# Cross-attention and expert feed-forward: the product with v in float32 on four 32-column strips, with a separate order of steps for each engine

## The chip, the core and the metric

The kernel runs on one core of a Trainium2 chip. The metric is the device time of one execution in microseconds (us). Engines are named as the profile names them: PE is TensorE (PEld its weight loads), DVE VectorE, ACT ScalarE, POOL GpSimd, SP SyncE, which here only issues DMAs (SPq). SBUF is the on-chip memory that all engines read, PSUM the banks that PE writes its results into.

## What is computed

There are 16 batches of 128 tokens of width 256, 2048 tokens in all. The reference, cut to what matters:

```python
# attention: 16 heads of width 16; one k and one v (each 128 x 16 per batch) shared by all heads
qh = (norm(x) @ w_q) ...;  k, v = split(ctx @ w_kv)
attn_prob = softmax(einsum('bhid,bjd->bhij', qh, k) / sqrt(16))
out = einsum('bhij,bjd->bhid', attn_prob, v);  x1 = x + out @ w_concat
# feed-forward on the normed x1: top-1 of 8 experts (256 -> 1024 -> 256), capacity 256 tokens,
# beside a residual MLP (256 -> 1024 -> 256) for every token, mixed by a softmax of two coefficients
out = res_mlp(a) * coef[:, :1] + moe(a) * coef[:, 1:] + residual
```

## The kernel before, in words

The tokens are worked in 8 units of 256 (two batches, t = 0 and 1), then the 8 experts follow. For every unit the kernel transposes ctx and the normed x (L586), makes kv and q (L591), splits q and k in three bfloat16 parts, sends them through DRAM to lie stacked (qstack, kstack), and computes the scores twice: A (L644, heads on the free axis, for the row maximum, which DVE reduces at L957) and B (L666, keys on the partitions, with the maximum subtracted by two added rows of the stack).

B comes in 8 groups per unit (g = 0 to 7; four heads and one batch each, one PSUM bank of 128 x 512). ACT takes the exponential of each group twice: in float16 into `p_hi` (L824) and in float32 into `p32` (L825; the profile calls it p). DVE subtracts the two into a float16 `p_lo` (L949, `low_part`). PE then multiplies p with v in `weigh` (L680 and L681): for each of the four heads of a group, `p_hi` and then `p_lo` is the stationary operand (128 x 128) and `vparts` the moving one, 49 columns wide (three bfloat16 parts of v and a column of ones, which gives the softmax's sum). Two groups fill one bank `pbank`; DVE takes the reciprocal of the ones' column (L973), sums the three parts (L974) and scales into `o_rows` (L977, function `o`). When the unit's four such pieces are done, PE transposes `o_rows` (oT, L586), ACT copies it, PE multiplies with w_concat (proj, L591 with wc), and DVE adds to x (L984), so that layer norm, gate and the residual MLP can follow.

The residual MLP of a unit (`up`, L591 with w1r, with the gelu on ACT at L860; `down`, L751 with w2r) runs one unit behind, between the attention steps of the next unit. A unit with such MLP work beside it is called loaded below (units 2 to 7 have nearly all of it). The experts have the same two products with w1e and w2e. Float32 products appear in the profile as two PE records for each 128 x 128 by 128 x 256 product, so that "x8" is four products.

All engines take their steps from one list, `plan`: each step has a time made of its unit's start (`OWN`, 32 apart from unit 3) and a phase from the tables `AT0`, `AT1` and `AT`, and the list sorted by time is the program order of each engine. The times are only for sorting. What really holds a step back are semaphores: `weigh` waits for `p_lo`; ACT's exponentials of group k wait for `p_lo` of group k-2 (L824, two buffers of `p32`); a PSUM bank is claimed again only when its last user has been read (`FREED`), and A and B share the two banks `sbank`.

Of the kernel before, what the change touches and what calls it, by code (L numbers as in the profile page):

```python
# [5 lines left out]
def xattn_moe_ffn_kernel(nc, x, ctx, w_q, w_kv, w_c, nw, nb, wg, inter_w, inter_b, output_w, output_b,  # L6
# [10 lines left out]
    P = 128  # L17
# [7 lines left out]
    T = 2  # L25
# [12 lines left out]
    NPS = 6  # L38
    VW = 3 * DH + 1
# [18 lines left out]
    OWN = [0.0, 14.83, 38.9, 67.3]  # L58
    while len(OWN) < U + 3:
# [3 lines left out]
        "load": [-77.76], "ln1": [-59.31], "xn": [-52.55], "ctxT": [-55.73], "xT": [-42.22], "kv": [-39.7],  # L63
        "q": [-39.27], "qrest": [-41.07], "qmid": [-34.81], "qlast": [-36.41], "vt": [-38.49],
        "A": [-16.51, -16.37, -14.32, -14.04, -12.48, -10.82, -10.55, -9.8], "M": [-12.87, -8.44],
        "B": [-1.47, -0.38, 0.52, 3.42, 7.22, 7.91, 10.76, 12.78],
        "low": [-0.31, 1.72, 3.41, 7.68, 9.19, 10.26, 11.63, 13.03],
        "PV": [4.6, 6.47, 8.23, 10.22, 11.82, 14.03, 15.29, 17.85], "o": [6.72, 9.53, 12.45, 15.99], "oT": [18.92],
        "proj": [20.34], "ln2": [22.4], "core": [23.87], "gate": [29.59], "loc": [37.82], "gw": [2.43],
        "bias": [12.71], "up": [18.3, 19.06, 22.25, 25.8],  # L70
        "down": [-1.64, -0.04, 0.29, 3.05, 5.91, 6.8, 10.19, 12.71], "kspill": [-35.6],
        "qspill": [-43.69, -43.49, -43.39], "gather": [-35.16, -34.04],
    }
    AT1 = {
        "load": [-99.55], "ln1": [-62.15], "xn": [-50.95], "ctxT": [-42.13], "xT": [-37.91], "kv": [-40.31],
        "q": [-34.66], "qrest": [-40.27], "qmid": [-28.41], "qlast": [-34.73], "vt": [-30.21],
        "A": [-19.69, -17.73, -15.68, -14.01, -13.84, -12.18, -11.91, -11.52], "M": [-10.41, -9.7],
        "B": [-0.63, 1.24, 4.13, 4.57, 7.09, 8.2, 10.89, 12.79],
        "low": [0.72, 2.0, 3.73, 7.82, 9.64, 10.74, 12.14, 13.85],
        "PV": [3.94, 5.82, 7.6, 9.61, 12.75, 13.45, 14.73, 17.31], "o": [6.44, 9.98, 13.29, 17.32], "oT": [18.38],  # L80
        "proj": [19.72], "ln2": [21.77], "core": [23.95], "gate": [26.61], "loc": [39.06], "gw": [14.41],
        "bias": [19.65], "up": [15.33, 16.98, 19.62, 23.21],
        "down": [-0.9, 1.35, 1.75, 5.08, 8.54, 10.31, 13.7, 20.67], "kspill": [-40.35],
        "qspill": [-42.52, -35.18, -34.88], "gather": [-34.05, -33.21],
# [13 lines left out]
    EARLY = 0.01  # L98
    LOADS = {
        "late": [-70.79], "vec": [-39.4], "zero": [-46.04, -45.13, -6.03, -0.66],  # L100
        "weights": [0.5, 14.17, 14.73, 27.03, 27.11],
    }

    HALVES = [T] + [1] * (U - 1)
# [1008 lines left out]
```

## Time and profile before

| | us |
|---|---|
| median of 3 runs (lowest, highest) | 441.46 (439.79, 446.71) |
| the profiled execution | 442.74 |
| its span, first to last instruction | 440.1 |
| PE busy (matmul records) | 372.5 |
| DVE busy | 202.7 |
| ACT busy | 190.1 |
| POOL busy | 158.2 |
| mean granted TensorE clock, share of full speed | 0.92 |

Busy time of PE counts a matmul until its last result has landed, which overlaps the next one. For what a matmul costs the queue, the distance between two starts is read, not the duration.

### The profile page before, as it was taken

To read this page: it belongs to the slowest core of one execution; us is meant where nothing else is said; L and a number is where in the kernel's file an instruction comes from. 1 tells how busy PE (TensorE), PEld (TensorE's weight loads), DVE (VectorE), ACT (ScalarE), POOL (GpSimd) and SP (SyncE) were. 2 spreads that over 40 slices of the span, in tenths; PEclk is the share of its full clock that TensorE was granted. 3 is DMA by queue.
4 is the path that set the end of the run, shared out by engine and by line. 5 is a ranking of instruction groups with operands and counts; after the bars stand their busy time and mean duration, and the time that the engine had idled before them with its cause. 6 is when DMAs were issued, how large, how long until landed. Compare 5 with 4: busy or idle time off the path is not lost. (4 is left out here: it accounts for less than half of the span.)

```text
span 440.1 us, 6595 instructions
## 1 busy us (share of the span) xinstructions
PE 372.5 (85%) x2298; PEld 298.4 (68%) x2298; DVE 202.7 (46%) x612; ACT 190.1 (43%) x373; POOL 158.2 (36%) x219
## 2 busy tenths in 40 slices
PE   4758676867998799899899879879999999999992
PEld 2435444655776677677677767768888888888881
DVE  3255778838545965965955957521001110101110
ACT  3213474557246646546546628443143322332210
POOL 4322134238174068168168061265002121212122
PEclk9865658989699999899899999989999999999997
DMA  6567670231023362472402400193213586571212
GB/s 200 182 181 218 216 184 18 74 82 38 15 72 116 98 227 74 113 255 75 106 24 73 108 26 15 42 370 92 56 41 96 167 246 189 136 220 13 24 18 30
DMA packets 51336, 49.84 MB, mean 113 GB/s; under 512 B 4764, under 2 KB 48488, under 8 KB 51304
## 3 DMA queue, kind: packets, MB, share of 16 engines
q1 hardware_dynamic: 48232, 45.21, 33.7%
q0 software_dynamic: 3072, 4.21, 5.2%
q8 instruction: 18, 0.29, 0.3%
q14 instruction: 14, 0.11, 0.1%
HBM read 33.65 MB, written 15.63 MB: 112 GB/s over the span
## 5 line engine op out<-in xcount | busy, mean ns | idle before, releaser
L860 ACT ACTIVATE h<-ubank,vecT 128x256 f32<-128x256 f32 x128 | 53.7, 471 | 129.3 <-PE ubank L591 129.1
L751 PE MATMUL mbank<-w2r,h 128*128 128x256 f32 x256 | 66.1, 399 | 0.5 <-ACT h L860 0.5
L591 PE MATMUL ubank<-ao,w1r 128*128 128x256 f32 x256 | 63.8, 396 | 0.0
L559 POOL DMA_INDIRECT out_rows<-yrow,rowid x16 | 24.8, 1550 | 103.3 <-DVE yrow L1078 73.2
L751 PE MATMUL mbank<-w2e,h 128*128 128x256 f32 x256 | 60.8, 379 | 0.0
L591 PE MATMUL ubank<-ao,w1e 128*128 128x256 f32 x256 | 60.0, 379 | 0.0
L751 PEld LDWEIGHTS mbank<-w2r,h 128*128 128x128 f32 x256 | 49.4, 198 | 7.6 <-issue 0.6
L591 PEld LDWEIGHTS ubank<-ao,w1r 128*128 128x128 f32 x256 | 49.5, 200 | 6.6
L591 PEld LDWEIGHTS ubank<-ao,w1e 128*128 128x128 f32 x256 | 48.5, 190 | 6.6
L751 PEld LDWEIGHTS mbank<-w2e,h 128*128 128x128 f32 x256 | 48.2, 190 | 6.3
L949 DVE TENSOR_TENSOR p_lo<-p,p_hi 128x512 f16<-128x512 f32 x64 | 46.4, 738 | 11.9 <-ACT p L825 11.7
L824 ACT ACTIVATE p_hi<-sbank 128x512 f16<-128x512 f32 x64 | 38.4, 600 | 30.1 <-PE sbank L666 17.5
L1074 DVE TENSOR_TENSOR ytmp<-mbank,outb 128x256 f32<-128x256 f32 x16 | 6.8, 425 | 90.9 <-PE mbank L751 90.9
L957 DVE TENSOR_REDUCE smax<-sbank 128x4 f32<-128x512 f32 x64 | 41.5, 682 | 11.6 <-PE sbank L644 9.8
L825 ACT ACTIVATE p<-sbank 128x512 f32<-128x512 f32 x64 | 38.4, 601 | 0.0
L680 PE MATMUL pbank<-vparts,p_hi 128*128 128x49 bf16 x256 | 24.0, 194 | 13.1 <-DVE p_lo L949 12.7
L644 PE MATMUL sbank<-kstack,qstack 96*128 96x128 bf16 x256 | 26.0, 244 | 10.7 <-ACT p L825 4.4
L680 PEld LDWEIGHTS pbank<-vparts,p_hi 128*128 128x128 f16 x256 | 19.1, 102 | 23.4 <-DVE p_lo L949 13.9
L644 PEld LDWEIGHTS sbank<-kstack,qstack 96*128 96x128 bf16 x256 | 19.0, 109 | 18.6 <-DVE smax L957 7.1
L666 PE MATMUL sbank<-qstack,kstack 98*128 98x512 bf16 x64 | 27.0, 431 | 4.0 <-DVE smax L957 2.6
L591 PE MATMUL mbank<-xT,wq 128*128 128x256 f32 x64 | 20.5, 476 | 4.0 <-ACT ao L841 3.0
L527 POOL TENSOR_TENSOR coef<-ge,grec 128x2 f32<-128x2 f32 x8 | 1.6, 202 | 61.6 <-DVE grec L1053 61.6
(127 smaller groups left out, 517.4 us busy)
## 6 DMA issues: line engine op xcount, KB each, us to landing
w1e<-in_L_ffn_inter_w SPq DMA_DIRECT2D x8, 1024.0 KB, 5.8
w2e<-in_L_ffn_output_w SPq DMA_DIRECT2D x8, 1024.0 KB, 8.8
qstack<-dram_q SPq DMA_DIRECT2D x16, 384.0 KB, 4.5
dram_q<-qpart SPq DMA_DIRECT2D x8, 384.0 KB, 2.6
dispatched<-zrow SPq DMA_DIRECT2D x4, 516.0 KB, 5.2
drow<-dispatched SPq DMA_DIRECT2D x8, 258.0 KB, 3.6
xs<-in_x SPq DMA_DIRECT2D x8, 256.0 KB, 3.4
ctxs<-in_ctx SPq DMA_DIRECT2D x8, 256.0 KB, 3.6
```

The costliest lines, as they stand in the source:

```text
L559: pool.indirect_dma_start(out=out[:, :], in_=yrow[:, e % 2, t, :], in_offset=None, compute_op=ALU.add, out_offset=bass.IndirectOffsetOnAxi ...
L591: last = nc.tensor.matmul(dst, w[kc], v[kc], start=(kc == 0), stop=(kc == len(w) - 1))
L644: last = nc.tensor.matmul(b[:, i * P:(i + 1) * P], qstack[0:KS, r, t, 4 * (g % HG) + i, :], kstack[0:KS, r, bs], start=True, stop=True)
L666: nc.tensor.matmul(b[:, :], kstack[:, r, bs], qstack[:, r, t, hs:hs + 4, :], start=True, stop=True)\
L680: nc.tensor.matmul(dst, p_hi[:, k % NPS, i, :], v, start=True, stop=False)
L751: last = nc.tensor.matmul(b[:, 0:D], h[:, n % 2, f, t * P:(t + 1) * P], w2[:, f, :], start=(f == 0), stop=(f == FC - 1))
L824: nc.scalar.activation(p_hi[:, k % NPS, :, :], scores, ACT.Exp, scale=SCALE).then_inc(sem("p_hi"), 1)
L825: nc.scalar.activation(p32[:, k % 2, :, :], scores, ACT.Exp, scale=SCALE).then_inc(sem("b_exp"), 1)
L860: nc.scalar.activation(h[:, n % 2, f, :], place["up", n, c][:, j, :], ACT.Gelu_apprx_tanh, bias=vecT[:, col:col + 1]).then_inc(sem("gelu_d ...
L949: V.tensor_tensor(p_lo[:, k % NPS, :, :], p32[:, k % 2, :, :], p_hi[:, k % NPS, :, :], ALU.subtract)\
L957: V.reduce_max(smax[:, g // HG, hs:hs + 4], place["A", u, g][:, :].rearrange("p (h t) -> p h t", h=4), AX)\
L1074: V.tensor_tensor(ytmp[:, t, :], b, outb[:, e, :], ALU.add).then_inc(sem("down_read"), 1)
```

## The change

The product with v no longer uses parts. ACT takes one exponential per group, in float32; `low_part` and its DVE subtraction are gone, as are the bfloat16 parts of v: `vone` holds v in float32, 32 columns wide (16 of v, one of ones, 15 of zeros). `weigh` is now called once per batch t, when its four groups of p are there: four float32 products, with `vone` (128 x 32) stationary and one group of p (128 x 512) moving, each at its own 32-column strip of the array (`tile_position=(0, 32 * g)`), so that group g's result lies in partitions 32g to 32g+31 of one bank. The result has head and token on the free axis. ACT copies it to `o_raw` (new step on ACT), and PE turns it back with four float32 transposes of 128 x 128 (new step `part`). DVE takes one reciprocal per batch and one multiplication straight from PSUM into `o_rows`. POOL's `bias` has one wait more, on a semaphore that POOL itself raises earlier in its order.

Besides, every engine sorts the list for itself: `order(lag)` adds to each kind of step a small number of that engine (`LAG_PE`, `LAG_ACT`, ...). A few phases in the tables are also changed; of the tables the diff below shows two lines.

```diff
-        "low": [-0.08, 0.18, 3.63, 7.8, 9.64, 10.74, 12.14, 13.57],
-        "PV": [4.11, 5.98, 7.74, 9.73, 12.42, 13.54, 14.8, 17.36], "o": [4.91, 9.92, 13.48, 16.76], "oT": [18.72],
+        "PV": [5.63, 14.29], "part": [7.43, 16.09], "o": [7.83, 16.49], "oT": [17.79],
...
-    plan = [step for _, _, step in sorted(steps)]
+    def order(lag):
+        return [step for _, _, step in sorted((place + lag.get(step[0], [0.0])[0], n, step) for place, n, step in steps)]
...
-                pe.wait_ge(sem("p_lo"), k + 1)
-                v = vparts[:, u % 3, g // HG, :]
-                for i in range(4):
-                    dst = b[:, 4 * (g % 2) + i, 0:VW]
-                    nc.tensor.matmul(dst, p_hi[:, k % NPS, i, :], v, start=True, stop=False)
-                    last = nc.tensor.matmul(dst, p_lo[:, k % NPS, i, :], v, start=False, stop=True)
+            def weigh(u, t):
+                n = T * u + t
+                pe.wait_ge(sem("b_exp"), HB * (n + 1))
+                if t == 0:
                     pe.wait_ge(sem("v_ready"), u + 1)
+                b = claim("PV", u, t)
+                for g in range(HB):
+                    last = nc.tensor.matmul(b[32 * g:32 * g + 32, :, :], vone[:, u % 3, t, :], p32[:, n % 2, g, :, :],
+                                            start=True, stop=True, tile_position=(0, 32 * g))
                 last.then_inc(sem("pv_done"), 1)
+
+            def o_part(u, t):
+                n = T * u + t
+                b = claim("part", u, t)
+                pe.wait_ge(sem("o_copied"), n + 1)
+                for i in range(HB):
+                    last = nc.tensor.transpose(b[:, i, :], o_raw[:, n % 2, i, :], ident[:, :])
+                last.then_inc(sem("o_turned"), 1)
...
-                if k >= 2:
-                    act.wait_ge(sem("p_lo"), k - 1)
-                if k >= NPS:
-                    act.wait_ge(sem("pv_done"), k - NPS + 1)
-                scores = place["B", u, g][:, :].rearrange("p (h t) -> p h t", h=4)
-                nc.scalar.activation(p_hi[:, k % NPS, :, :], scores, ACT.Exp, scale=SCALE).then_inc(sem("p_hi"), 1)
-                nc.scalar.activation(p32[:, k % 2, :, :], scores, ACT.Exp, scale=SCALE).then_inc(sem("b_exp"), 1)
+                if k >= 2 * HB and g % HB == 0:
+                    act.wait_ge(sem("pv_done"), k // HB - 1)
+                scores = place["B", u, g][:, :].rearrange("p (h t) -> p h t", h=HB)
+                nc.scalar.activation(p32[:, (k // HB) % 2, g % HB, :, :], scores, ACT.Exp, scale=SCALE)\
+                    .then_inc(sem("b_exp"), 1)
+
+            def o_copy(u, t):
+                n = T * u + t
+                act.wait_ge(sem("pv_done"), n + 1)
+                if n >= 2:
+                    act.wait_ge(sem("o_turned"), n - 1)
+                copy(o_raw[:, n % 2, :, :], place["PV", u, t][:, :, :]).then_inc(sem("o_copied"), 1)
...
-            def low_part(u, g):
-                k = G * u + g
-                dve.wait_ge(sem("b_exp"), k + 1)
-                dve.wait_ge(sem("p_hi"), k + 1)
-                V.tensor_tensor(p_lo[:, k % NPS, :, :], p32[:, k % 2, :, :], p_hi[:, k % NPS, :, :], ALU.subtract)\
-                    .then_inc(sem("p_lo"), 1)
...
-                own(V.reciprocal(o_rec[:, r, :], bank[:, :, VW - 1]))
-                V.tensor_reduce(o_sum[:, r, :, :], bank[:, :, 0:3 * DH].rearrange("p h (a d) -> p h d a", a=3), AX,
-                                ALU.add).then_inc(sem("o_summed"), 1)
-                dve.wait_ge(sem("o_summed"), G // 2 * u + b + 1)
-                V.tensor_tensor(o_rows[:, t, r * P:(r + 1) * P].rearrange("p (h d) -> p h d", d=DH),
-                                o_sum[:, r, :, :], o_rec[:, r, :].unsqueeze(2).broadcast_to([P, NH // 2, DH]), ALU.mult)\
+                b = place["part", u, t][:, :, :].rearrange("p i (j x) -> p j i x", j=HB)
+                V.reciprocal(o_rec[:, :, :], b[:, :, :, DH]).then_inc(sem("o_root"), 1)
+                dve.wait_ge(sem("o_root"), n + 1)
+                V.tensor_tensor(o_rows[:, t, :].rearrange("p (j i d) -> p j i d", j=HB, i=HB), b[:, :, :, 0:DH],
+                                o_rec[:, :, :].unsqueeze(3).broadcast_to([P, HB, HB, DH]), ALU.mult)\
                     .then_inc(sem("o_ready"), 1)
```

The first place is PE in a steady unit, where the scores B (`sbank<-qstack,kstack`) alternate with the MLP's second product (`mbank<-w2r,h`). Before, with only the first pair of the product with v of a group of four pairs:

```order
L666 MATMUL sbank<-qstack,kstack 128x512
L680 MATMUL pbank<-vparts,p_hi 128x49
L681 MATMUL pbank<-vparts,p_lo 128x49
...
L666 MATMUL sbank<-qstack,kstack 128x512
L751 MATMUL mbank<-w2r,h 128x256 x2
L680 MATMUL pbank<-vparts,p_hi 128x49
L681 MATMUL pbank<-vparts,p_lo 128x49
```

and now, from the last two scores of the first batch to those of the second:

```order
L687 MATMUL sbank<-qstack,kstack 128x512 x2
L776 MATMUL mbank<-w2r,h 128x256 x2
L697 MATMUL pbank<-p,vone 32x512 x4
L687 MATMUL sbank<-qstack,kstack 128x512
L776 MATMUL mbank<-w2r,h 128x256 x2
L706 MATMUL pbank<-ident,o_raw 128x128 x4
...
L687 MATMUL sbank<-qstack,kstack 128x512
L697 MATMUL pbank<-p,vone 32x512 x4
L776 MATMUL mbank<-w2r,h 128x256 x2
L665 MATMUL sbank<-kstack,qstack 128x128 x8
```

Eight small pieces of the product with v, one after each group, have become two large ones, each behind the last group of its batch, and each followed by a set of transposes after one or two other steps.

The second place is ACT in the same unit: before (four of the eight pairs),

```order
L824 ACT_TABLE_LOAD
L824 ACTIVATE p_hi<-sbank 128x512
L825 ACTIVATE p<-sbank 128x512
...
L850 ACTIVATE ge<-gd 128x20
L860 ACT_TABLE_LOAD
```

and now:

```order
L847 ACT_TABLE_LOAD
L847 ACTIVATE p<-sbank 128x512 x4
L791 ACTIVATE o_raw<-pbank 128x512
L847 ACTIVATE p<-sbank 128x512 x4
L791 ACTIVATE o_raw<-pbank 128x512
L880 ACTIVATE ge<-gd 128x20
L890 ACT_TABLE_LOAD
```

Sixteen exponentials have become eight, and two copies have come in between; the copy of the first batch stands in front of the exponentials of the second, and the copy of the second in front of the gelu of the MLP.

## Rows read from the trace of the kernel before

**Rows 1.** Busy time by stretch: engine busy (instructions), PEclk, DMA share, GB/s.
```profile
core 0: us, PE busy (x) PEld busy (x) DVE busy (x) ACT busy (x) POOL busy (x), PEclk, DMA share, GB/s
...
40.00:67.00 27.00, 20.11 (x142) 12.71 (x141) 17.66 (x41) 14.77 (x29) 7.26 (x8) 0.58 0.74 219
...
91.00:131.00 40.00, 32.11 (x220) 25.29 (x219) 23.35 (x74) 21.21 (x39) 22.39 (x33) 0.87 0.20 55
...
163.00:195.00 32.00, 28.78 (x214) 22.60 (x212) 22.20 (x69) 17.90 (x35) 16.93 (x24) 0.95 0.49 152
195.00:227.00 32.00, 28.86 (x216) 22.91 (x215) 21.97 (x67) 18.65 (x36) 16.59 (x24) 0.95 0.25 71
...
308.00:440.00 132.00, 121.77 (x576) 105.81 (x574) 14.41 (x41) 35.06 (x81) 24.80 (x16) 0.98 0.40 103
```

**Rows 2.** PE's timeline, projection of units 3, 4 and 6: start us, us.
```profile
157.16 1.95 PE L591 MATMUL mbank<-wc,oT 128*128 128x256 f32 x8
...
190.20 1.95 PE L591 MATMUL mbank<-wc,oT 128*128 128x256 f32 x8
...
254.45 1.95 PE L591 MATMUL mbank<-wc,oT 128*128 128x256 f32 x8
```

**Rows 3.** PE's timeline in unit 5: start us, us, records, [idle before <-releaser].
```profile
202.41 1.06 PE L591 MATMUL mbank<-wg_raw,ao 128*128 128x10 f32 x8
203.33 1.11 PE L751 MATMUL mbank<-w2r,h 128*128 128x256 f32 x4
...
211.07 0.19 PE L680 MATMUL pbank<-vparts,p_hi 128*128 128x49 bf16 x1
...
211.27 0.38 PE L666 MATMUL sbank<-qstack,kstack 98*128 98x512 bf16 x1
211.49 1.03 PE L751 MATMUL mbank<-w2r,h 128*128 128x256 f32 x4
213.64 0.18 PE L680 MATMUL pbank<-vparts,p_hi 128*128 128x49 bf16 x1 [1.13 <-DVE p_lo L949]
...
215.02 0.20 PE L680 MATMUL pbank<-vparts,p_hi 128*128 128x49 bf16 x1 [0.80 <-DVE p_lo L949]
...
220.44 0.61 PE L644 MATMUL sbank<-kstack,qstack 96*128 96x128 bf16 x8
220.89 0.61 PE L586 MATMUL mbank<-ident,o_rows 128*128 128x128 f32 x4
221.34 1.89 PE L591 MATMUL ubank<-ao,w1r 128*128 128x256 f32 x8
223.07 0.39 PE L644 MATMUL sbank<-kstack,qstack 96*128 96x128 bf16 x4
```

**Rows 4.** PE's groups: busy us, mean ns | idle before, us, by releaser.
```profile
L644 PE MATMUL sbank<-kstack,qstack 96*128 96x128 bf16 x256 | 26.0, 244 | 10.7 <-ACT p L825 4.4 <-DVE smax L957 3.6 <-DMA qstack<-dram_q 2.1
L680 PE MATMUL pbank<-vparts,p_hi 128*128 128x49 bf16 x256 | 24.0, 194 | 13.1 <-DVE p_lo L949 12.7
...
L591 PE MATMUL mbank<-xT,wq 128*128 128x256 f32 x64 | 20.5, 476 | 4.0 <-ACT ao L841 3.0 <-ACT xT L766 0.8 <-issue 0.2
...
L591 PE MATMUL mbank<-ctxT,wkv 128*64 128x256 f32 x32 | 10.9, 475 | 1.4 <-ACT ctxT L766 1.4
```

**Rows 5.** DVE's groups, the same columns.
```profile
L949 DVE TENSOR_TENSOR p_lo<-p,p_hi 128x512 f16<-128x512 f32 x64 | 46.4, 738 | 11.9 <-ACT p L825 11.7
...
L974 DVE TENSOR_REDUCE o_sum<-pbank 128x128 f32<-128x384 f32 x32 | 16.1, 503 | 0.0
...
L977 DVE TENSOR_TENSOR o_rows<-o_sum,o_rec 128x128 f32<-128x128 f32 x32 | 9.6, 301 | 1.1
```

**Rows 6.** ACT's groups, the same columns.
```profile
L825 ACT ACTIVATE p<-sbank 128x512 f32<-128x512 f32 x64 | 38.4, 601 | 0.0
L824 ACT ACTIVATE p_hi<-sbank 128x512 f16<-128x512 f32 x64 | 38.4, 600 | 30.1 <-PE sbank L666 17.5 <-issue 11.9 <-DVE p_lo L949 0.4
...
L766 ACT ACTIVATE oT<-mbank 128x512 f32<-128x512 f32 x8 | 4.8, 597 | 3.0 <-PE mbank L586 2.8
```

More of the change, by code:

```diff
@@ L106, in xattn_moe_ffn_kernel @@
         "period": 17.22, "up": [-2.35, 2.53, 4.67, 9.02],
-        "down": [17.14, 18.77, 20.43, 21.32, 23.56, 25.83, 26.3, 28.47], "ein": [9.47], "first": [-3.51],
+        "down": [17.16, 18.79, 20.45, 21.34, 23.58, 25.85, 26.32, 28.49], "ein": [9.47], "first": [-3.51],
     }
@@ L130, in xattn_moe_ffn_kernel @@
             add(OWN[u] + at["M"][i], "M", u, i + HALVES[u] - T)
-        for kind in ("A", "B", "low", "PV", "o"):
+        for kind in ("A", "B", "PV", "part", "o"):
             for i, phase in enumerate(at[kind]):
@@ L264, in xattn_moe_ffn_kernel @@
         ubank = [ex.enter_context(nc.psum_tensor(f"ubank{i}", [P, 2, UT], f32)) for i in range(2)]
-        pbank = [ex.enter_context(nc.psum_tensor(f"pbank{i}", [P, NH // 2, 64], f32)) for i in range(2)]
+        pbank = [ex.enter_context(nc.psum_tensor(f"pbank{i}", [P, HB, P], f32)) for i in range(2)]
         sems = {}
@@ L306, in uses @@
             if kind == "PV":
-                return [("p", "PV", k[0], k[1] // 2)] if k[1] % 2 == 0 else []
+                return [("p", "PV") + k]
+            if kind == "part":
+                return [("p", "part") + k]
             return []
         place, before_it, held = {}, {}, {ring: [] for ring in RING}
-        for step in plan:
+        for step in order(LAG_PE):
             for ring, *key in uses(*step):
@@ L438, in _ @@
                      "down": down, "end": end}
-            for step in plan:
+            for step in order(LAG_SP):
                 if step[0] in calls:
@@ L568, in _ @@
                      "gw": scatter, "bias": bias, "down": down, "end": end}
-            for step in plan:
+            for step in order(LAG_POOL):
                 if step[0] in calls:
@@ L756, in _ @@
             calls = {"vec": vectors, "ctxT": tr_ctx, "xT": tr_x, "kv": kv, "q": q, "vt": vt, "A": score_max,
-                     "M": max_rows, "B": scores_T, "PV": weigh, "oT": oT, "proj": proj, "core": cT, "gate": lg,
+                     "M": max_rows, "B": scores_T, "PV": weigh, "part": o_part, "oT": oT, "proj": proj, "core": cT, "gate": lg,
                      "loc": loc, "ein": ein, "up": up, "down": down}
-            for step in plan:
+            for step in order(LAG_PE):
                 if step[0] in calls:
```

120 lines of the change are left out of this document (61 added, 59 removed), and 6 rows, old and new, of tables (AT, AT0, AT1).

## The prediction

> **What bounds the kernel now.** I read the busy time by stretch first [rows 1]. In the expert stage (308 to 440) PE is busy 121.77 of 132 us and DVE and ACT are nearly idle; the change touches nothing there, so whatever it is worth arises before 308. In the steady units (163 to 227) PE is busy 28.8 of 32 us, DVE 22, ACT 18. Early on (40 to 67) PE's clock is 0.58 of full, DVE has 17.66 of 27 us and ACT 14.77: there no engine is full, and chains of waits set the pace.
>
> A busy PE is not a full PE, so next I count what a loaded unit takes of PE's queue, from distances between starts [rows 3]. Eight float32 records of 256 columns start over 1.73 us (221.34 to 223.07), 0.216 us each; a unit has 84 of them (32 up, 32 down, 8 q, 8 projection, 4 kv): 18.1 us. Eight groups of B at 0.22 (211.27 to 211.49) are 1.8. Two groups of A take 0.45 (220.44 to 220.89), eight 1.8. A set of four transposes takes 0.45 (220.89 to 221.34), and there are four sets: 1.8. The gate takes 0.9 (202.41 to 203.33), small things some 0.3. The product with v takes 0.20 per group (211.07 to 211.27, eight matmuls), 1.6 per unit. Sum: 26.3 us. The projection of unit 3 starts at 157.16 and that of unit 6 at 254.45 [rows 2], so a unit takes 32.4 us. PE therefore loses 6.1 us per unit in waits and at half clock (the two steady stretches have a mean clock of 0.95; a tenth of the time at half speed costs up to 1.6 us of 32).
>
> Where does it lose them? At the product with v above all: PE waits 13.1 us at L680 over the run, 12.7 of it for `p_lo`, and 4.4 at L644 for ACT's second exponential [rows 4]. In unit 5 two such waits show 1.13 and 0.80 us, and each is really longer by about 0.16, because a matmul's record (0.18) outlasts its place in the queue (0.025) [rows 3]. I put 3.0 us of a unit's 6.1 at these places; about 3.1 lie elsewhere.
>
> **The change part by part.** *Removed.* PE: 64 small matmuls, -1.6 us per unit. ACT: 64 exponentials of 600 ns, -38.4 us over the run [rows 6]. DVE: 64 subtractions, -46.4, and the sums of the parts, -16.1; the scalings go from 32 of 301 ns to 16 larger ones read from PSUM, about even [rows 5]. DVE and ACT aren't full in the steady units, so this counts only through PE's waits: the chain from a group of scores to its product was exponential, exponential, subtraction (0.6 + 0.6 + 0.74) and becomes one exponential.
>
> *Added on ACT.* 16 copies of 128 x 512; the copy of oT, of the same shape, takes 597 ns: 9.6 us over the run [rows 6]. A copy waits for the product with v, and four exponentials (after the first) or the gelus (after the second) are queued behind it. Between product and transposes PE has a group of B and two records' worth of other work or more (0.22 + 0.86 us, from starts 0.22 and 0.216 apart), against 0.16 + 0.60 and two semaphores for the copy: I cost it at nothing. Without this cover it would be about 0.9 us, twice per unit.
>
> *Added on PE: transposes.* Two sets of four at 0.45: +0.9 us per unit [rows 3].
>
> *Added on PE: the strips.* This term decides. A group is one product of 512 columns in float32, two records, each twice as long as one of 256 columns (0.216): 0.43. That the stationary operand is narrow saves nothing by itself: kv's product with 64 columns has a mean of 475 ns, q's with 128 has 476 [rows 4]. So a batch, four strips and eight records, takes 8 x 0.43 = 3.45 us if the strips run one after another. If all four run at once it is 2 x 0.43 = 0.86. No row shows two strips at work together. Between the ends lies a third value. Both records of a product need the same strip, so the second must follow the first; and PE's records start in the order of the program everywhere in the timeline. Then the first record of strip 1 can run beside the second of strip 0, and so on: 5 x 0.43 = 2.15 us per batch. I take this one, 4.3 us per unit, and keep 1.7 and 6.9 as ends.
>
> [...]
>
> *Change of array shape.* Going into and out of the strips may cost PE a pause, four times a unit. The trace has nothing like it; below by 0, above by one matmul's tail, 0.16 each, 0.6 per unit. I take 0.3. [...]
>
> *Waits that remain at the product.* Before each batch's product PE waits for the last exponential: from the start of a group of B, 0.38 until it is done, 0.6 for ACT, 0.1 for semaphores, less what PE does meanwhile (0.22, or 0.22 + 0.86): about 0.9 for the second batch and 0.3 for the first, 1.2 per unit. They replace the 3.0.
>
> *A loaded unit:* -1.6 + 0.9 + 4.3 + 0.3 - 3.0 + 1.2 = +2.1 us. Six of them: +12.6.
>
> *Half clock.* It stands behind PE's waits for `p_lo` in both steady stretches [rows 1]. With fewer waits and more matmul time some of it goes: up to 1.6 us in each of the two, and more in 91 to 131 (mean 0.87). I take -4 (0 to -7).
>
> *Units 0 and 1.* Here DVE and ACT carry the chains. Per unit 8 x 0.74 of DVE and 8 x 0.60 of ACT go, 10.7 us of work, while PE gets its longer product at about half clock, 2 x (4.3 - 0.8) us, in a stretch where it has room. Net per unit -2.5 (between -5 and +3): -5.
>
> *The orders.* DVE loses some 8 us of work per unit, so the maxima and layer norms that PE waits for (3.6 us at L644 alone [rows 4]) come sooner; the new tables shift steps by tenths of a microsecond. No row prices that: nothing at one end, those 3.6 us and as much again at other places at the other. I take -4.
>
> *Sum:* 12.6 - 4 - 5 - 4 = -0.4. Against the profiled execution's 442.74 us, of which 440.1 are span and 2.6 lie around it, this gives 442.3; that run was 1.3 above the median of the runs shown, so 441.0. No change that a measurement would tell: 2% is 8.8 us, about what the measurement of this kernel can tell from none.
>
> **The rivals.** *All strips at once.* A batch takes 0.86 and not 2.15: 2.6 us per unit less, and +2.1 becomes -0.5. Six units: -3; clock -4, early units -6 and orders -4 as above; the sum is -17 and the time 425. As less of PE's work is then there to cover the copy and the chains of layer norm and gate, I give back 3: 428. For it speaks that four strips share no cell of the array and write different partitions; against it, that the second record of a product has to follow its first. No row decides it. [...]
>
> *Strips one after another*, the case in which the change doesn't do what it says. A batch takes 3.45: +1.3 twice, +4.7 per unit, but longer products also cover waits (-0.5): +4.2 x 6 = 25. Early units +2 (their products at half clock are 6.9 us each, and ACT's copy with the exponentials behind it waits for them), clock -2, orders -4: +21, 463. It decides from about 2.7 us per batch on: then PE's added work outweighs all that the waits gave. For it speaks that every product in the trace runs alone.
>
> *ACT's queue turns into the wait.* If the copy comes late, PE stands at the transposes and the exponentials behind it come late too: 0.9 us twice per unit over six units, +11 on my sum: 452. Against it: ACT is busy 18 of 32 us.
>
> **How the numbers follow.** My forecast 0.40, all at once 0.32, one after another 0.18, ACT's queue 0.10. Of the forecast (433 to 450) 0.05 is faster by over 2%, 0.31 within, 0.04 slower. All at once gives 0.28 faster and 0.04 within; one after another 0.17 slower, 0.01 within; ACT's queue 0.06 slower, 0.04 within. Together: faster 0.33, same 0.40, slower 0.27. The forecast's own range is 433 to 450; with the other cases the range is 424 to 463.
>
> **What would show it.** In the profile after: starts of the eight records of a batch's product. Mine: the pairs overlap, some 2.15 us from the first to the next instruction; 0.86 or 3.45 would show a rival. The transposes' wait for ACT's copy should be near nothing; the wait at L680 (13.1) should shrink to some 1.2 us per unit; the projections of units 3 to 6 should lie about 32 us apart; the expert stage should keep its 132 us. The prediction is wrong if a batch's product isn't near 2.15, or if the units shorten though it is.

## The result, and the profile after

The change made no difference of 2%: the kernel after takes 444.89 us (median of 20 runs, 443.27 to 448.85), the kernel before 443.46 (20 runs, 438.38 to 451.54). The ratio is 1.0085, with a 95% interval of 1.0055 to 1.0115, so it is a little slower, and not faster. The ratios here leave out executions more than 1.5% above the fastest of their kernel, seven of the 20 of before and none of after; by the medians of all 20 the kernel after is 0.3% slower. I had forecast 441.0, that is 442.3 for the profiled execution; that one took 447.72, with a span of 446.0. The profiled execution after lies 2.8 us above its own median, the one before 0.7 below, so of the 5.0 us between the two profiled executions only 1.4 are left between the medians. What follows is therefore read from stretches at full clock, not from the spans alone.

The answer to [rows 1] and to the totals:

```profile
core 0: us, PE busy (x) PEld busy (x) DVE busy (x) ACT busy (x) POOL busy (x), PEclk, DMA share, GB/s
40.00:67.00 27.00, 20.50 (x88) 9.53 (x86) 9.21 (x25) 9.50 (x18) 6.91 (x9) 0.68 0.67 198
91.00:131.00 40.00, 33.93 (x185) 25.92 (x184) 15.92 (x58) 17.54 (x31) 18.96 (x29) 0.87 0.20 55
163.00:195.00 32.00, 28.40 (x176) 21.15 (x174) 16.10 (x51) 16.01 (x30) 16.53 (x24) 1.00 0.38 119
195.00:227.00 32.00, 28.40 (x169) 20.76 (x168) 14.85 (x50) 16.01 (x30) 14.63 (x23) 0.95 0.35 103
```
```profile
PE 381.6 (86%) x1978; PEld 292.7 (66%) x1978; DVE 142.2 (32%) x461; ACT 167.6 (38%) x325; POOL 153.2 (34%) x219
```

DVE lost 60 us of work over the run (202.7 to 142.2) and ACT 22 (190.1 to 167.6), as the diff says. In the steady stretches DVE went from 22 to 15 or 16 us of 32. Neither was the bound, and the time did not follow them.

The product with v is what my forecast turned on. PE's timeline in unit 5 of the kernel after (start us, us, records, [idle before <-releaser]), to be laid beside [rows 3]:

```profile
213.67 1.03 PE L776 MATMUL mbank<-w2r,h 128*128 128x256 f32 x4
214.79 1.06 PE L697 MATMUL pbank<-p,vone 128*32 128x512 f32 x8
215.78 0.39 PE L687 MATMUL sbank<-qstack,kstack 98*128 98x512 bf16 x1
216.01 1.03 PE L776 MATMUL mbank<-w2r,h 128*128 128x256 f32 x4
216.88 0.60 PE L706 MATMUL pbank<-ident,o_raw 128*128 128x128 f32 x4
...
219.58 0.38 PE L687 MATMUL sbank<-qstack,kstack 98*128 98x512 bf16 x1
220.65 1.06 PE L697 MATMUL pbank<-p,vone 128*32 128x512 f32 x8 [0.69 <-ACT p L847]
221.64 1.13 PE L776 MATMUL mbank<-w2r,h 128*128 128x256 f32 x4
```

A batch's product, four strips and eight records, takes 0.99 us from its first start to the next instruction (214.79 to 215.78, 220.65 to 221.64; the raw starts give 0.998 and 0.995). It is neither my 2.15 nor the serial 3.45. The raw starts of the eight records in this batch are 214.787, 214.793, 214.800 and 214.807, and then 215.240, 215.247, 215.253 and 215.260: the first records of all four products, 7 ns apart, then the second records of all four. (The records name no strip; that they divide like this is read from the run with one strip below.)

So PE's work per unit grew by only -1.6 + 0.9 + 2 x 0.99 = +1.3 us. Yet a steady unit at full clock became longer. Before, the projections of units 5 and 6 start at 223.29 and 254.45: 31.16 us, a unit without a half-clock stretch. (The 32.4 us of my forecast was a mean over three units, two of which have one.) After, with the places of the waits:

```profile
159.29 1.97 PE L612 MATMUL mbank<-wc,oT 128*128 128x256 f32 x8 [0.62 <-ACT oT L791]
192.25 1.97 PE L612 MATMUL mbank<-wc,oT 128*128 128x256 f32 x8 [0.57 <-ACT oT L791]
226.90 1.97 PE L612 MATMUL mbank<-wc,oT 128*128 128x256 f32 x8 [0.57 <-ACT oT L791]
```

From 226.90 to the next projection at 259.87 it is 32.97 us, 1.8 more than before. (From 159.29 to 259.87 it is 33.5 on the average, where I had expected about 32.) PE's waits by what was waited for (us in total, times, longest) show a new one, for ACT's copy of oT, which had stood nowhere in PE's groups before:

```profile
PE mbank L607 <- DVE core L1021: 10.3, 8, 3.3
PE pbank L697 <- ACT p L847: 7.8, 9, 1.8
PE sbank L665 <- DVE smax L977: 6.7, 9, 2.1
...
PE mbank L612 <- ACT oT L791: 4.2, 6, 1.1
```

Against [rows 4], the product's waits have fallen from 13.1 to about 8 us, but those for the maxima at A have grown from 3.6 to 6.7, and 4.2 us for oT are new. The timeline after shows why. After the last product, PE now runs through this piece of its order:

```profile
225.26 0.63 PE L607 MATMUL mbank<-ident,o_rows 128*128 128x128 f32 x4
225.72 0.61 PE L665 MATMUL sbank<-kstack,qstack 96*128 96x128 bf16 x8
226.90 1.97 PE L612 MATMUL mbank<-wc,oT 128*128 128x256 f32 x8 [0.57 <-ACT oT L791]
228.71 1.89 PE L612 MATMUL ubank<-ao,w1r 128*128 128x256 f32 x8
230.43 0.61 PE L665 MATMUL sbank<-kstack,qstack 96*128 96x128 bf16 x8
231.61 0.40 PE L665 MATMUL sbank<-kstack,qstack 96*128 96x128 bf16 x4 [0.56 <-DVE smax L977]
231.84 0.61 PE L607 MATMUL mbank<-ident,ctxs 128*128 128x128 f32 x4
...
236.54 0.63 PE L607 MATMUL mbank<-ident,core 128*128 128x128 f32 x4 [0.69 <-DVE core L1021]
```

Between the transposes of o_rows and the projection stand only two groups of A (0.45 us), too little to cover ACT's copy of 0.6 us (0.597 in [rows 6]); before, eight records of the up-projection (1.73 us) and one group of A stood there [rows 3]. And with the projection earlier, twelve matmuls of A (three groups, on two banks) follow in a row, so PE waits for a maximum. DVE, whose order is fixed too, adds a delay of its own (same columns; L1003 adds to x, L1021 makes core):

```profile
228.91 0.69 DVE L1003 TENSOR_TENSOR xs<-xs,mbank 128x512 f32<-128x512 f32 x1 [1.47 <-PE mbank L612]
230.86 1.29 DVE L977 TENSOR_REDUCE smax<-sbank 128x4 f32<-128x512 f32 x2 [1.27 <-PE sbank L665]
232.06 0.74 DVE L926 BATCH_NORM_STATS2 stats<-xs 128x6 f32<-128x256 f32 x2
...
234.44 0.69 DVE L977 TENSOR_REDUCE smax<-sbank 128x4 f32<-128x512 f32 x1 [0.49 <-PE sbank L665]
235.05 1.35 DVE L1021 TENSOR_SCALAR core<-xs,mv,yy 128x256 f32<-128x256 f32 x2
```

The layer norm of the new x waits behind maxima whose scores come later: from the addition to x to the second core it takes 6.6 us (228.91 to 235.51; the raw start of the second is 235.51). In the kernel before it took 4.1 (225.27 to 229.33). The two instructions for core also last longer here, 0.54 and 0.88 us against 0.40 and 0.41 before; what that goes with shows further down. So the order of the steps, which I had put down as a gain of 4 us, became the suspect.

### The profile page after: what moved, and what is told of

Its sections match the earlier page's. It is cut to its first block, busy times and chain, and to the rows that moved or that the text cites. A ratio compares the mean times of both kernels' runs of the same rounds, so it can differ in the third digit from the quotient of the medians.

```text
span 446.0 us, 5656 instructions
## 1 busy us (share of the span) xinstructions
PE 381.6 (86%) x1978; PEld 292.7 (66%) x1978; DVE 142.2 (32%) x461; ACT 167.6 (38%) x325; POOL 153.2 (34%) x219
## 4 chain that ended last, share of the span: by engine, by line
PE 65%; DMA 10%; ACT 8%; DVE 7%; issue 5%; POOL 2%; SPq 2%; DVEq 0%; POOLq 0%; ACTq 0%
PE mbank L776 20%; PE ubank L612 18%; PE mbank L612 11%; DMA drow<-dispatched 8%; PE mbank L607 4%; PE pbank L697 4%; ACT p L847 3%; PE sbank L665 3%; PE sbank L687 3%; DVE smax L977 3%; PE pbank L706 2%; DVE core L1021 2%; ACT h L890 1%; DMA wq_raw<-in_L_xattn_w_q 1%; ACT oT L791 1%
## 5 line engine op out<-in xcount | busy, mean ns | idle before, releaser
L776 PE MATMUL mbank<-w2r,h 128*128 128x256 f32 x256 | 64.1, 390 | 0.5 <-ACT h L890 0.5
L612 PE MATMUL ubank<-ao,w1r 128*128 128x256 f32 x256 | 62.7, 393 | 0.0
L776 PEld LDWEIGHTS mbank<-w2r,h 128*128 128x128 f32 x256 | 48.4, 194 | 12.8 <-issue 5.3
L847 ACT ACTIVATE p<-sbank 128x512 f32<-128x512 f32 x64 | 36.9, 595 | 33.8 <-PE sbank L687 33.7
L687 PE MATMUL sbank<-qstack,kstack 98*128 98x512 bf16 x64 | 25.0, 418 | 2.2 <-DVE smax L977 1.8
L697 PE MATMUL pbank<-p,vone 128*32 128x512 f32 x128 | 19.1, 671 | 8.2 <-ACT p L847 7.8
L871 ACT ACTIVATE ao<-mbank,vecT 128x256 f32<-128x256 f32 x32 | 16.3, 561 | 15.3 <-PE mbank L607 15.3
L529 POOL TENSOR_TENSOR yy<-va,mhalf 128x4 f32<-128x4 f32 x8 | 8.4, 1046 | 39.7 <-DVE va L1012 39.7
L612 PE MATMUL mbank<-wc,oT 128*128 128x256 f32 x64 | 18.0, 429 | 4.2 <-ACT oT L791 4.2
L496 POOL TENSOR_TENSOR rs<-va,mhalf 128x2 f32<-128x2 f32 x8 | 5.8, 720 | 45.7 <-DVE va L936 45.7
```

What stands on the lines that cost most here:

```text
L612: last = nc.tensor.matmul(dst, w[kc], v[kc], start=(kc == 0), stop=(kc == len(w) - 1))
L687: nc.tensor.matmul(b[:, :], kstack[:, r, bs], qstack[:, r, t, hs:hs + 4, :], start=True, stop=True)\
L697: last = nc.tensor.matmul(b[32 * g:32 * g + 32, :, :], vone[:, u % 3, t, :], p32[:, n % 2, g, :, :], start=True, stop=True, tile_position= ...
L776: last = nc.tensor.matmul(b[:, 0:D], h[:, n % 2, f, t * P:(t + 1) * P], w2[:, f, :], start=(f == 0), stop=(f == FC - 1))
L847: nc.scalar.activation(p32[:, (k // HB) % 2, g % HB, :, :], scores, ACT.Exp, scale=SCALE)\
L871: ins = nc.scalar.activation(ao[:, n % NAO, kc, :], place["cT", n][:, kc * UT:(kc + 1) * UT], ACT.Identity, bias=vecT[:, R_NB + kc:R_NB + ...
```

## The experiments

Two theories stood at the start. Theory S: the strips' product is what keeps the gain away. Theory O: the strips are cheap and the new order, above all the earlier projection, costs it. All ratios are against the kernel before, run on the same chip.

### What the strips cost

*The product issued twice* (after, `for g in list(range(HB)) * 2`).

> The changed kernel with each batch's four strip products issued twice (the second set writes the same values over the first; the work is doubled, the output is the same). If PE's queue sets the pace wherever the product stands, 16 times 0.85 us more, plus half as much again in the early units at half clock: +15 us over the changed kernel, 460. If the product stood in slack: under +5.

Measured: 457.33 us, ratio 1.040 (1.031 to 1.048), span 457.3. PE's timeline:

```profile
218.73 1.92 PE L697 MATMUL pbank<-p,vone 128*32 128x512 f32 x16
220.58 0.39 PE L687 MATMUL sbank<-qstack,kstack 98*128 98x512 bf16 x1
```

Sixteen records take 1.85 us in place of 0.99: four more products cost 0.86, once more two records of 512 columns (0.429 each here) for all four strips together. Sixteen batches at 0.86 are 13.8; the span grew by 11.3, since some of it lies in the early units, where PE has room.

*No strips* (v padded with zeros to the full width of the array, four products summed in one bank; the same output, everything else as after).

```diff
-                    last = nc.tensor.matmul(b[32 * g:32 * g + 32, :, :], vone[:, u % 3, t, :], p32[:, n % 2, g, :, :],
-                                            start=True, stop=True, tile_position=(0, 32 * g))
+                    last = nc.tensor.matmul(b[:, :, :], vone[:, u % 3, t, g, :], p32[:, n % 2, g, :, :],
+                                            start=(g == 0), stop=(g == HB - 1))
```

> The changed kernel without strips: v stands zero-padded in a 128 x 128 stationary operand, once for each group, and the four products of a batch are summed in the same bank; three small DVE copies more per unit. By the trace of the changed kernel the four strips run together (0.99 us a batch, first to next instruction); one after another they take 8 x 0.43 = 3.45. Both theories: 16 x 2.45 = +39 us, more in the units at half clock: 484 to 492. If it is under +15, the strips weren't what made the product short.

Measured: 482.49 us, ratio 1.097 (1.083 to 1.111), just under the expected range. The timeline:

```profile
231.60 3.70 PE L697 MATMUL pbank<-p,vone 128*128 128x512 f32 x8
235.13 0.38 PE L687 MATMUL sbank<-qstack,kstack 98*128 98x512 bf16 x1
```

This is my serial end, as a measurement: 3.53 us per batch. It also prices the change of array shape. In the strips, the last record starts at 215.260 and the next instruction at 215.785, 0.525 later; here the last record's start (205.165) is 0.43 before the next. Leaving the strips thus costs 0.10 us. Entering costs nothing that shows: from the start of the four records ahead to the product it is 1.12 us with strips (213.67 to 214.79) and 1.12 without (230.475 to 231.596). But in both PE has waited some 0.26 us for the exponentials there, so a price of entering that fits into such a wait would not show.

*One strip of the four* (after; from unit 2 on `for g in (HB - 1,)`).

> The changed kernel, but from unit 2 on only one of a batch's four products with v is issued (the last strip's); the other three strips of the bank keep what unit 0 or 1 left there, so three quarters of the attention output are not computed. Twelve batches are touched. All together (the strips stream at the same time, as the raw starts of a batch's eight records say): a batch's product falls from 0.99 us only to 0.85 to 0.95, and the time by 0 to 3 us, 442 to 446. Staggered (my forecast, 2.15 us a batch): 12 x 1.29 = 15 us less, 429 to 431. One after another (3.45): 12 x 2.6 = 31 us less, 413 to 416.

Measured: 444.99 us (444.68 to 451.04), ratio 1.010 (1.000 to 1.020), level with after's 444.89. The timeline:

```profile
209.09 1.05 PE L697 MATMUL pbank<-p,vone 128*32 128x512 f32 x2
210.07 0.39 PE L687 MATMUL sbank<-qstack,kstack 98*128 98x512 bf16 x1
```

Its two records start at 209.089 and 209.543, 0.454 us apart, and last 0.617 and 0.592 us, as each record of the first and of the second set of four does in after. One strip takes 0.98 us, four take 0.99 (I had expected 0.85 to 0.95 for the one: the 0.10 of leaving the strips is there whether one or four were used). Three of the four products cost 0.01 us together: the strips work side by side. Theory S is out, and so are my forecast's mechanism and the serial rival.

### What the order costs

*The old order* (after's computation; the steps common to both kernels have before's phases in one list, with no lags for single engines; the new steps stay at after's places).

> The changed kernel's computation with the phases of the kernel before for all steps that both have, one list for all engines and no lags; the product with v, its transposes and the scaling at the changed kernel's places. Theory O: the old order has the projection behind an up-step and none of PE's wait for the copy, so 4 us less than the changed kernel, 441, below the kernel before or equal to it. Theory W: 445 or more, since what the tables changed is small beside the chain.

*The same kernel again*, with more executions.

> The changed computation in the old order once more, for a narrower interval against the kernel before. The computation alone is worth what this gives: the ratio was 0.988 with an interval of 0.974 to 1.002. Theory (a steady unit at full clock is level with before, 31.1 against 31.16 us, and the 6.5 us come from units 0 to 2 and from three half-clock windows fewer after 160): 434 to 438 us, ratio 0.980 to 0.992. Rival (that one profile was lucky in its clock and the computation is worth nothing): ratio 0.992 to 1.002.

Measured: 435.6 us (432.3 to 440.43), ratio 0.988 (0.974 to 1.002), and again 433.5 us (432.77 to 436.92), ratio 0.982 (0.975 to 0.989). That is 5 us below what I had expected of it. By the ratios the computation alone is worth 5 to 8 us; the order that came with it costs 9 to 11 (444.89 less 435.6 or 433.5). A steady unit is 31.1 us (projections at 184.02 and 215.11), level with the 31.16 of before. PE's timeline of it, first run, answers to the piece shown above:

```profile
183.80 0.39 PE L644 MATMUL sbank<-kstack,qstack 96*128 96x128 bf16 x4
184.03 1.95 PE L591 MATMUL mbank<-wc,oT 128*128 128x256 f32 x8
185.81 0.61 PE L644 MATMUL sbank<-kstack,qstack 96*128 96x128 bf16 x8
186.26 0.61 PE L586 MATMUL mbank<-ident,ctxs 128*128 128x128 f32 x4
186.70 1.89 PE L591 MATMUL ubank<-ao,w1r 128*128 128x256 f32 x8
188.69 0.40 PE L644 MATMUL sbank<-kstack,qstack 96*128 96x128 bf16 x4
...
190.61 0.63 PE L586 MATMUL mbank<-ident,core 128*128 128x128 f32 x4
```

No wait of half a microsecond is left in this stretch: none for oT, none for the maxima, none for core. The gain against before is already 4.2 us at the addition to x of unit 3 (159.15 before, 154.91 here), and at unit 6 it is 8.2 (256.43 against 248.20). This run has no half-clock stretch between 160 and 250 where before has two, of 3.4 us, at 181.9 and 216.0; at half speed each costs up to 1.7 us, 3.4 of the 4.0 that came in between.

*Which part of the order?* First the narrow guess: from unit 3 on only the projection moved back, to phase 19.6, behind one more up-projection.

> The changed kernel; from unit 3 on the projection stands one up-step later in PE's order (phase 19.6 and not 18.79). Theory O (the new order gives the time back): PE's wait of 0.57 us for ACT's copy of oT goes, and as the layer norm's last step waits for a maximum anyway, nothing comes in its place: 5 units x 0.7 = 3.5 us less than the changed kernel (444.9), about 441.5. Theory W (the unit is a chain whose length the product sets, and PE has more work): the wait moves to the transposes of the normed x, time as the changed kernel's within 1 us.

Measured: 448.59 us (446.05 to 452.86), ratio 1.025 (1.013 to 1.036), slower than after. The wait for oT was gone, but PE waited 0.94 us for a maximum (0.56 in after) and still 0.69 for core; the first steady unit took 32.6 us, and once a transfer of qstack was waited for, 3.5 us. The theory in this narrow form fell: the wait was passed on, not removed.

*The copy and the projection both back at before's phases*, in all three tables, everything else as after.

```diff
-        "PV": [5.63, 14.29], "part": [7.43, 16.09], "o": [7.83, 16.49], "oT": [17.79],
-        "proj": [18.79], "ln2": [21.72], "core": [23.76], "gate": [30.12], "loc": [39.86], "gw": [16.86],
+        "PV": [5.63, 14.29], "part": [7.43, 16.09], "o": [7.83, 16.49], "oT": [18.72],
+        "proj": [21.09], "ln2": [21.72], "core": [23.76], "gate": [30.12], "loc": [39.86], "gw": [16.86],
```

> The changed kernel with one thing of its order undone: the copy of o and the projection stand at the phases that they had before (18.72 and 21.09, in place of 17.79 and 18.79). The computation is the changed one in full. Theory P (the place of the projection is what the order costs: twelve groups of A in a row wait for smax, wc waits for ACT's copy of o, and the core of the next unit stands behind smax of the last A): a steady unit goes from 32.97 us to 31.0 to 31.4, the waits of L612 for oT fall from 4.2 us to under 1 and those of L607 for the core from 10.3 to 5 to 8, and the time is 434 to 437 us, 8 to 11 below the changed kernel. Rival Q (the loss is spread over the other changed numbers, the lags of the engines or the place of the exponentials): the unit stays at 32.3 or more and the time at 441 to 446.

Measured: 439.54 us (435.0 to 441.07), ratio 0.990 (0.982 to 0.998), 5.4 us below after's median. The span is 437.2, 8.8 under after's, but after's profiled execution lay 2.8 above its own median. The unit is 31.36 us as expected; the time missed the expected 434 to 437. PE's waits:

```profile
PE mbank L607 <- DVE core L1021: 12.4, 8, 3.3
PE pbank L697 <- ACT p L847: 7.2, 8, 2.1
PE sbank L665 <- DVE smax L977: 4.7, 5, 2.4
```

The waits for oT are gone (4.2) and those for the maxima down by 2. Of core I had expected less, and it rose: the core of a steady unit is now 4.2 us behind the addition to x (219.92 to 224.11) and not 6.6, but that addition itself comes later in the unit, and PE still waits 0.62 there. What makes the steady unit 1.6 shorter are the two other waits. Counted from starts each is 0.73 in after (225.72 + 0.45 to 226.90, 230.43 + 0.45 to 231.61), more than the idle 0.57 and 0.56 of the rows, since a record outlasts its place in the queue (0.61 us against 0.45 for eight records of A).

*The mirror*: the old order, with only these two steps at after's phases.

> The mirror of the run before: the changed computation in the old order (435.6 us), where only the copy of o and the projection are moved to the changed kernel's phases (17.79 and 18.79). Theory P: the unit goes from 31.1 to 32.5 to 33.2 us, waits of L612 for oT of 3 us or more come up, and the time is 441 to 446 us. Rival Q: 434 to 438 us, unit within 0.4 of 31.1.

Measured: 443.89 us (440.92 to 448.0, 10 runs), ratio 1.000 (0.996 to 1.004), span 442.1 against 433.6 without the move, unit 32.35. The waits for oT are back (4.2 us, 6 times, just as in after), as here in PE's timeline:

```profile
190.09 1.97 PE L591 MATMUL mbank<-wc,oT 128*128 128x256 f32 x8 [0.56 <-ACT oT L770]
```

The unit came out a little under the 32.5 that I had expected at the least. By medians the two steps cost 8 to 10 us in the old order (443.89 against 435.6 and 433.5) and give 5.4 back in the new one; by spans it is 8.5 and 8.8.

*The rest of the new order, on before's computation* (old product, parts and projection; after's numbers and lags for the rest).

> The kernel before (p and v in two bf16 parts, its product and projection at their own phases), with the changed kernel's numbers and lags for all steps that the two have in common. Theory P: those numbers matter little once product and projection stand where they stood: 440 to 447 us, within 1% of before. Rival Q: they cost what the changed kernel lacks against the old order, 448 to 455 us.

Measured: 440.94 us (438.08 to 448.08), ratio 0.997 (0.992 to 1.002): in time it neither costs nor gains anything that shows. In a steady unit it does cost. Here the projections of units 4 and 5 start 32.61 us apart, with no half-clock stretch between 114 and 431, against 31.16 in the kernel before:

```profile
188.03 1.95 PE L615 MATMUL mbank<-wc,oT 128*128 128x256 f32 x8
...
194.89 0.63 PE L610 MATMUL mbank<-ident,core 128*128 128x128 f32 x4 [0.62 <-DVE core L1026]
...
220.64 1.95 PE L615 MATMUL mbank<-wc,oT 128*128 128x256 f32 x8
```

PE waits longer for `p_lo` in such a unit (2.7 us against 1.1) and, as in after (0.69) and with the two steps back (0.62), for core. Before, the old order and its mirror have no such wait of half a microsecond. In the three kernels that have it, DVE's two instructions for core take 0.54 to 0.88 us each in a steady unit, and POOL works at the bias while they run, as in after:

```profile
234.51 0.93 POOL L566 TENSOR_SCALAR rbias<-resb,coef 128x256 f32<-128x256 f32 x1
```

In the other three (before, the old order, its mirror) they take 0.40 to 0.41 us, and POOL is idle then. So this wait comes with the rest of the new order and not with the two steps; that POOL's work is what makes core longer is not tested. In time the kernel before loses elsewhere what it saves there: it has three half-clock stretches between 160 and 300 and this run has none.

What is shown, then: the place of the copy of o and the projection costs 8 to 10 us in the old order and 5.4 in the new one. The rest of the new order is small, but not nothing: with the two steps back the changed kernel's 439.54 is 4 to 6 us above the old order (435.6 and 433.5), though the intervals of the ratios touch, and its unit 0.26 longer (31.36 against 31.10).

*Early or steady units?* The same undoing in the steady table alone (units 2 to 7), and in the two early tables alone.

> The changed kernel with the old phases of the copy of o and the projection in the table for units 2 to 7 alone; units 0 and 1 keep the new ones. By the starts of the additions to x, the two earlier places cost 5.4 us of the 8.8 before unit 2 was through (92.33 against 86.96) and the steady units 1.6 us each. If the early units' loss passes on to the end: the addition to x of unit 1 stays near 92.3, the unit is 31.4, and the time is 439 to 443. Rival: units 0 and 1 catch up while they wait for other things, and the time is that of the full undoing, 437 to 440.

> The complement: the old phases of the copy of o and the projection for units 0 and 1 alone, the new ones from unit 2. If the early units' gain stays to the end: the addition to x of unit 1 at 87, a unit of 33.0 from there, and 440 to 444. Rival (the gain is lost again before the loaded units begin): within 1.5 us of the changed kernel, 444 to 447.

Measured: steady alone 445.83 us (439.87 to 447.73, 4 runs), ratio 1.001 (0.987 to 1.014); early alone 437.75 (435.36 to 442.01), ratio 0.988 (0.979 to 0.998). The first can't be told from anything: its interval holds both the full gain and none. Its profiled execution is at the low end, with the unit of 31.4 us that was expected. The second did more than either line expected. Because the projection's place in the unit differs, I compare where DVE makes the second core of unit 7: 294.48 after, 285.60 steady alone, 286.22 early alone, 283.72 both. Taken as they are, each half alone gives 8 to 9 of 10.8 us.

But the profiled execution of after is a poor measure here. Up to 130 us TensorE's granted clock is at half (0.50 of full speed) for 61.4 us in it (from 16.1 for 23.9 us, from 46.8 for 17.1, and four shorter stretches). In the run with one strip, which has the same order and a product only 0.01 to 0.02 us shorter, it is 47.8, as much as in early alone (from 18.2 for 20.5 us, from 45.5 for 17.1, and three of 3.4) and in steady alone. That run has its second core of unit 7 at 288.63. Against it the leads are 3.0, 2.4 and 4.9 us, and the 4.9 fit the 5.4 between the medians. Steady alone shows the same: its units 0 and 1 are those of after, and yet its addition to x of unit 1 is at 88.93 and not near the expected 92.3. So both halves give something, the early one 4.4 us by the second core of unit 2 (129.46 against 133.84).

In the old order the division can be read as well: the move of the two steps puts the projection of unit 3 4.8 us later (157.74 against 152.92) and that of unit 6 8.9 (255.08 against 246.21), with 54.6 us at half clock up to 130 against 44.4. How much of the early part is clock, and whether the clock follows from the order, is left open.

### A version that beats both

*Old order, and from unit 3 on two steps moved behind the work that PE waited in front of*: `AT3 = dict(AT, q=[-37.8], PV=[5.63, 14.6])`.

> The changed computation in the old order, and from unit 3 on two steps of TensorE moved: the projection of q stands one up-projection later (it waited 1.0 us a unit for ao), and the products of the strips one down-projection later (the first waited 0.85 us for its exponentials). Theory P, which says that in the steady units the time is TensorE's issue plus the waits at a few fixed places: the unit goes from 31.1 to 29.3 to 30.3 us and the time to 426 to 432 us, faster than both. Rival R (these waits only pass to the next wait, as the one for the copy of o passed to the core when the projection alone was moved): the unit stays at 30.8 or more and the time at 434 to 437 us.

Measured: 436.63 us (429.86 to 440.32, 6 runs), ratio 0.976 (0.968 to 0.983); the ratio is of the three executions up to 435.90, whose median is 431.88. It is faster than both kernels, but not told apart from the old order by itself (0.982, 0.975 to 0.989). PE's waits for ao and p in a steady unit, here of the kernel after (226.9 to 259.87; the old order has the same two):

```profile
PE mbank L612 <- ACT ao L871: 1.0, 1, 1.0
PE pbank L697 <- ACT p L847: 0.7, 1, 0.7
```

And all of PE's waits in a steady unit of this version (217.8 to 248.47):

```profile
PE mbank L592 <- DVE qres L934: 1.2, 1, 1.2
PE pbank L686 <- ACT o_raw L771: 0.2, 1, 0.2
```

The profiled execution took 437.36 us, above the median. The waits for ao and p are gone, and PE waits 1.2 us for DVE's residual of q and 0.2 for the copy of o_raw instead; the unit is 30.67, 0.4 shorter than 31.1 where 1.7 us of waits had been aimed at. That is the rival's mechanism, with a small gain left.

## Why the prediction was wrong

**What bounds it, and the stage.** Right. The expert stage hardly moved (from the last addition to x of the eight units to the end 156.3 us before, 155.2 after), DVE and ACT gave up 60 and 22 us at no direct profit, and the matter was decided by PE's work and waits before 308.

**The strips: +4.3 per unit.** This is the first step that failed. I said: "Both records of a product need the same strip, so the second must follow the first", and from PE's starts in program order I made a staircase of 5 x 0.43. A product's second record does come 0.45 us after its first, but the staircase does not follow from it: the records of four products in a row on four strips do not come as pairs. The four first ones start within 20 ns, 7 ns apart, and the four second ones 0.45 us later. PE's starts in program order, which I had read in the trace of before, I took as an order of records, and that is not what the records show. Why the second records stand behind all the first ones no run shows. It is 0.99 us per batch, 2.0 per unit and not 4.3, as one strip against four (0.98 and 0.99), the doubled product (+0.86) and the full array (3.53) show. The rival "all at once" had this right.

**Change of shape: +0.3 per unit.** Measured 0.10 per batch, only on leaving: 0.2, and contained in the 2.0. The 0.10 us on leaving (0.525 against 0.429) is all that shows of such a price here, since before entering PE had waited some 0.26 us for the exponentials. The 0.3 was my estimate, with no row behind it that shows a pause. The 0.2 stands in the lower part of my 0 to 0.6.

**Transposes +0.9, old product -1.6.** Right. ACT's copy at nothing: right in the steady units (no wait at L706 in unit 5); over the run 1.9 us, which also rules out the rival of ACT's queue.

**Waits at the product: -3.0 and +1.2.** What remains was right: in unit 5 it is 0.26 and 0.85, 1.1 in all. What went was oversized. The clean unit of before loses 1.9 us there; the 3.0 was a share of 6.1 that I had spread by feel over a mean with half clock in it.

With the measured terms the unit is -1.6 + 0.9 + 2.0 - 1.9 + 1.1 = +0.5, and half a microsecond less waiting at A (0.46 us at 249.14 before, not there in the old order) brings it to the 31.1 against 31.16 that was measured. So in the steady units this computation is worth nothing at full clock. What it earns lies in the early units (predicted -5; 4.2 by unit 3 in the old order) and in half-clock stretches (predicted -4). The two aren't cleanly apart: up to 130 us the old order has 44.4 us at half clock and the kernel before 54.6. Between 160 and 300 the old order has one or two stretches of 3.4 us, before three, and the kernel after one, but its first units had more. That half clock stands behind the waits for `p_lo`, as I had it, [rows 1] does not show. The trace of before has the two side by side (PE waits 1.12 us up to 180.59 and half clock begins at 181.9; 1.13 up to 213.64 and 0.80 up to 215.02, and it begins at 216.0). That fewer waits leave less half clock, on which the -4 rested, was my estimate; no run shows it, and one speaks against it: the rest of the new order on before's computation has more of these waits (14.8 us against 12.7) and no half-clock stretch between 114 and 431.

**The orders: -4, "nothing at one end".** This is the second step that failed; it hid the first, and it alone turned the sign, as the old order shows (0.982 and 0.988 of before). I gave a range from nothing to a gain, and never one of loss. The two steps' move, which the order of instructions had shown, costs 8 to 10 us by medians in the old order and 5.4 in the new, and the new order as a whole 9 to 11. The reading that would have priced it was open to me: a copy of 597 ns on ACT [rows 6] behind the transposes, and 0.45 us of work in place of 1.73 + 0.22 to cover it. I had applied exactly this test to the new copy and not to the old one that had been moved. It prices the wait for oT alone, 4.2 us of the run.

**The sum.** My forecast lay 4 us under the median, and that is luck: strips too dear by 2.3 per unit (14 us over six), and order too cheap by 13 to 15. The rival "all at once" at 428 had the mechanism, and missed by the order; its own figure with the order term at zero, 432, is what the old order gave (433.5). (The serial rival's 463 is 21 above the 442 of the profiled execution, while my 441 and the 452 count from the median: a slip of 1 us.)

## What to carry to other kernels

Small float32 products on four column strips (here 128 x 32 stationary, 512 columns moving), issued one after another, cost PE as much as one of them (0.99 us against 0.98): count a set of four as one product of two records. When a change comes with a new order, cost the order by itself: for each step that moved, the work that now stands between it and its producer must be as long as the producer takes on its engine (here 0.45 us stood against a copy of 0.60), and each maximum or copy that now stands ahead of a layer norm in another engine's order delays it (here from 4.1 to 6.6 us between the addition to x and the core). A wait that is taken away at one place often passes to the next one, and only the length of the whole unit tells whether anything was won.

## What the runs showed of the hardware

- The two records of a float32 product do not start as a pair when the products that follow lie in other strips: first records at 214.787, .793, .800, .807 and second ones at 215.240, .247, .253, .260; alone in its strip, a product has its two records at 209.089 and 209.543. In the full array (L697 in the run without strips) the second and later records follow 0.429 us apart.
- Coming out of the strips to a product of the full array costs 0.10 us (0.525 against 0.429 from the last record to the next instruction), going in nothing that shows beside a wait of 0.26 us.
- DVE's instruction for core (128 x 256, float32) took 0.40 to 0.41 us in a steady unit where POOL was idle, and 0.54 to 0.88 where POOL worked at the bias beside it. No run changed this alone.
- Programs that are the same differ from one execution to the next in where the half-clock stretches fall. Up to 80 us the kernel after has 47.8 us of it in its profiled execution (from 16.1 for 23.9, 46.8 for 17.1, 70.7 for 6.8), and the run with one strip, which is the same program up to unit 2, has 37.5 (from 25.3 for 10.2, 42.4 for 23.9, 69.7 for 3.4). Its span was 3.1 us shorter, while the medians are equal (444.99 and 444.89). A single profile's span is no measure for a change of this size.
